# A transformer decoder layer on one core: q and k transposed without stacking, their rows spread by DMA inside SBUF

## What is computed

```python
x = x + attn(layernorm(x), Wqkv, Wo)          # rope on q and k, causal, 16 heads
x = x + xattn(layernorm(x), ctx, mask)        # softmax(x ctx^T / 16) ctx
x = x + ffn(layernorm(x), gate, w1, w2, w3, sw1, sw2, sw3)

q, k = rope(q), rope(k)                       # r0 = x0 cos - x1 sin, r1 = x0 sin + x1 cos
scores = where(causal, q k^T / sqrt(16), -inf)
out = softmax(scores) v
```

## Time and profile before

| | us |
|---|---|
| runs, median of 3 | 271.58 |
| runs, lowest to highest | 269.91 to 271.66 |
| profiled execution, span from first to last instruction | 271.7 |
| TensorE busy in it | 259.4 |
| ScalarE, VectorE, GpSimd busy | 174.8, 170.0, 122.4 |

### The profile page before, as it was taken

The page is one execution under the profiler, slowest core; times in us unless marked ns, Lnnn a source line. Parts: engine busy times, 40 slices in busy tenths (PEclk is TensorE's granted clock), DMA queues, the critical chain, the costliest instruction groups (busy, mean ns, idle before and its releaser), DMA issues.

```text
span 271.7 us, 4900 instructions
## 1 busy us (share of the span) xinstructions
PE 259.4 (95%) x1805; PEld 210.2 (77%) x1810; DVE 170.0 (63%) x361; ACT 174.8 (64%) x292; POOL 122.4 (45%) x133
## 2 busy tenths in 40 slices
PE   7888989999999999999989999999999999999994
PEld 2447756768877787868778888888989898888884
DVE  3675886867778666776852579638446634545453
ACT  7479379889967799888888855627565313222230
POOL 4447454988776918990954780334320000000000
PEclk9997999999999999999999999999999999999999
DMA  7891000000000000006609600000000079000002
GB/s 235 328 397 70 1 5 2 0 5 0 2 0 0 5 0 4 1 5 229 195 12 249 170 0 4 2 0 2 0 0 2 14 230 255 6 0 4 0 0 78
DMA packets 11879, 17.08 MB, mean 63 GB/s; under 512 B 1904, under 2 KB 8272, under 8 KB 11856
## 3 DMA queue, kind: packets, MB, share of 16 engines
q1 hardware_dynamic: 11856, 16.78, 19.6%
HBM read 15.63 MB, written 1.08 MB: 62 GB/s over the span
## 4 chain that ended last, share of the span: by engine, by line
PE 71%; POOL 8%; DMA 6%; DVE 6%; issue 4%; ACT 3%; SPq 2%; DVEq 0%; ACTq 0%
PE bank L789 26%; PE bank L898 13%; PE bank L802 11%; PE bank L951 4%; DMA res<-x 4%; POOL prob_lo L419 3%; DMA w_raw<-w 3%; PE bank L843 3%; PE bank L796 2%; PE bank L829 2%; PE bank L867 2%; PE bank L822 2%; PE bank L847 2%; POOL w_lo L426 1%; PE bank L824 1%
## 5 line engine op out<-in xcount | busy, mean ns | idle before, releaser
L419 POOL TENSOR_TENSOR prob_lo<-prob,prob_hi 128x1536 f16<-128x1536 f32 x16 | 49.9, 3120 | 14.9 <-ACT prob_hi L542 14.8
L789 PE MATMUL bank<-x_hi,w_hi 128*128 128x512 f32 x112 | 45.5, 406 | 0.0
L789 PE MATMUL bank<-x_hi,w_lo 128*128 128x512 f32 x112 | 44.2, 395 | 0.0
L789 PE MATMUL bank<-x_lo,w_hi 128*128 128x512 f32 x112 | 44.1, 393 | 0.0
L615 DVE TENSOR_REDUCE negm<-bank 128x2 f32<-128x512 f32 (+1 forms) x48 | 31.6, 685 | 8.6 <-PE bank L824 6.6
L771 DVE TENSOR_TENSOR h_lo<-h_c,h_hi 128x512 fp32r<-128x512 f32 x28 | 23.6, 845 | 21.0 <-ACT h_hi L581 20.8
L581 ACT CAST h_hi<-h_c 128x512 fp32r<-128x512 f32 x28 | 17.3, 617 | 24.6 <-DVE h_c L766 17.1
L757 DVE TENSOR_TENSOR h_c<-bank,h_s 128x512 f32<-128x512 f32 x28 | 19.3, 688 | 21.9 <-PE bank L789 18.3
L898 PE MATMUL bank<-w_hi,h_hi 128*128 128x256 f32 x112 | 32.9, 294 | 0.1
L575 ACT ACTIVATE h_s<-bank 128x512 f32<-128x512 f32 x28 | 16.7, 596 | 24.7 <-PE bank L789 24.7
L898 PE MATMUL bank<-w_hi,h_lo 128*128 128x256 f32 x112 | 31.6, 283 | 0.0
(11 more groups left out here) (128 smaller groups left out, 573.3 us busy)
## 6 DMA issues: line engine op xcount, KB each, us to landing
w_raw<-w SPq DMA_DIRECT2D x3, 1792.0 KB, 8.2
comb_b<-comb_dram SPq DMA_DIRECT2D x8, 256.0 KB, 4.9
res<-x SPq DMA_DIRECT2D x4, 256.0 KB, 7.0
ctxt_s<-ctx_t SPq DMA_DIRECT2D x4, 256.0 KB, 7.5
ctx_s<-ctx SPq DMA_DIRECT2D x4, 256.0 KB, 7.4
out<-res SPq DMA_DIRECT2D x8, 128.0 KB, 1.8
comb_b<-comb_dram SPq DMA_DIRECT2D x4, 224.0 KB, 4.8
wqkv_s<-wqkv SPq DMA_DIRECT2D x1, 768.0 KB, 4.8
```

The lines of the kernel that those rows point to most:

```text
L419: eng.tensor_tensor(prob_lo[:, b % 2], prob[:, b % 2], prob_hi[:, b % 2], ALU.subtract)\
L789: ins = pe.matmul(dst, a(k), c(k), start=(k == 0 and i == 0), stop=(k == kt - 1 and i == 2))
```

## The change

A tile's `rot` is transposed as it is: its 512 columns give four transposes instead of sixteen, into one PSUM bank (step `tr`, now one per tile). ScalarE casts that bank once to the high part `qk_hi`, VectorE subtracts once for the low part `qk_lo` (step `kt`). The steps `sh` are gone on both engines, and so is `stk`. To spread the rows into the stacked buffers, SP issues nine DMAs inside SBUF (step `sk`, function `shuffle`): six for q (16 partitions each) and three for k (32 each), six of the nine from the high part. `sk.0` and `sk.1` move a tile each of batch 0, `sk.2` to `sk.4` a whole batch each of batches 1 to 3. The maxima products of a batch now wait for all nine (`qk_in`), and w3's load for the last two moves. The columns of Wq and Wk are put in another order on the host so that a head's channels come out as `shuffle` needs them, and the rope products follow that order. A pair of heads takes 96 rows instead of 112. The row of ones in `k_t` is written once by a DMA. The diff, cut to its core; of the lists only SP's:

```diff
-SHIFT = SLOT + KROWS
+SHIFT = 2 * KROWS
+PIECES = ((0, 0), (1, 1), (2, 0)), ((0, 0), (1, 0), (2, 1))
+MOVES = 9
...
     "SP": """
-        ln1.0 mt.0 mt.1 mt.2 mt.3 mt.4 ct.0 mt.5 w3.0 ct.1 ro.0 ro.1 cb.0 ct.2 ct.3 y.0 cb.1 y.1
+        x.1 x.2 w1.0 w2.0 sk.0 sk.1 x.3 wo.0 cx.0 mt.0 cx.1 mt.1 sk.2 gt.0 mt.2 sk.3 ro.0 mt.3 sk.4 mt.4 ro.1 ct.0
+        w3.0 mt.5 ct.1 cb.0 ct.2 y.0 ct.3 cb.1 y.1
...
+            def shuffle(g):
+
+                b, tok = (0, slice(g * P, (g + 1) * P)) if g < NT else (g - 1, slice(0, S))
+                tile = g if g < NT else NT * b + 1
+                if g == 0:
+                    sp.wait_ge(s["zero_ok"], 2)
+                elif g == NT:
+                    sp.wait_ge(s["zero1_ok"], 2)
+                if b >= 2:
+                    sp.wait_ge(s["s_ps"], 3 * NG * (b - 1))
+                for low, src, ok in ((0, qk_hi, "hi_ok"), (1, qk_lo, "lo_ok")):
+                    sp.wait_ge(s[ok], tile + 1)
+                    for r in range(2):
+                        for a, piece in PIECES[0]:
+                            if piece == low:
+                                row = 2 * DH * a + DH * r
+                                sp.dma_start(q_t[row:row + DH, b % 2, :, r, tok].bitcast(F32),
+                                             src[P // 2 * r:P // 2 * (r + 1), b % 2, 0:2, tok].bitcast(F32))\
+                                    .then_inc(s[f"qk_in{g}"], 16)
+                    for a, piece in PIECES[1]:
+                        if piece == low:
+                            row = 2 * DH * a
+                            sp.dma_start(k_t[row:row + 2 * DH, b % 2, :, tok].bitcast(F32),
+                                         src[:, b % 2, 2:4, tok].bitcast(F32)).then_inc(s[f"qk_in{g}"], 16)
...
-                    sp.wait_ge(s["st_ps"], 4 * NT * B)
+                    sp.wait_ge(s["qk_in3"], 16 * MOVES)
+                    sp.wait_ge(s["qk_in4"], 16 * MOVES)
                     sp.dma_start(w3_raw[:], w3.rearrange("(f p) c -> p f c", p=P)).then_inc(s["w3_in"], 16)
...
+                    act.copy(qk_hi[:, n // NT % 2, :, n % NT * P:(n % NT + 1) * P],
+                             ps_st[n % 2][:].rearrange("p (g q) -> p g q", g=4)).then_inc(s["hi_ok"], 1)
...
+                    dve.wait_ge(s["hi_ok"], n + 1)
+                    dst = (slice(None), n // NT % 2, slice(None), slice(n % NT * P, (n % NT + 1) * P))
+                    dve.tensor_tensor(qk_lo[dst], ps_st[n % 2][:].rearrange("p (g q) -> p g q", g=4),
+                                      qk_hi[dst].bitcast(F32), ALU.subtract).then_inc(s["lo_ok"], 1)
...
-                    for j in range(4):
-                        h = 8 * c + 2 * j
-                        ins = pe.transpose(ps_st[c % 2][:, j * P:(j + 1) * P],
-                                           stk[:, n % 2, h:h + 2, :].bitcast(F32).rearrange("p h r -> p (h r)"), ident[:])
+                    for c in range(4):
+                        ins = pe.transpose(ps_st[n % 2][:, c * P:(c + 1) * P],
+                                           rot[:, n % 2, 2 * c:2 * c + 2].rearrange("p g a i -> p (g a i)"), ident[:])
...
                     if b == 0:
-                        pe.wait_ge(s["qt_ok"], 2)
-                        pe.wait_ge(s["kt_ok"], 2)
+                        pe.wait_ge(s["qk_in0"], 16 * MOVES)
...
                     elif b % FILLS == 0:
+                        pe.wait_ge(s[f"qk_in{b // FILLS + 1}"], 16 * MOVES)
+                        pe.wait_ge(s["lo_ok"], NT * (b // FILLS + 1))
```

More of the change, by code:

```diff
@@ L62 @@
+        ln3.3 w3.11 w3.12 w3.13
     """,
     "ACT": """
[L64 to L67, removed]
@@ new lines @@
+        m.15 s.8 s.9 m.16 m.17 pv.0 m.18 m.19 s.10 s.11 m.20 m.21 pv.1 m.22 m.23 mt.2 early.1 pv.2 tr.4 tr.5 s.12 pv.3
+        s.13 s.14 v.2 s.15 ot.0 s.16 s.17 wo.0 s.18 m.24 m.25 s.19 s.20 m.26 pv.4 m.27 m.28 t2.0 xt.3 m.29 xs.0 m.30
+        qk.6 pt.0 m.31 m.32 ro.0 s.21 m.33 s.22 s.23 pv.5 m.34 m.35 qk.7 mt.3 t3.0 tr.6 pv.6 late.1 lg.0 s.24 s.25
+        tr.7 pv.7 s.26 v.3 ct.0 s.27 ot.1 s.28 s.29 wo.1 s.30 pv.8 s.31 m.36 m.37 s.32 m.38 m.39 t2.1 m.40 m.41 xs.1
+        s.33 m.42 s.34 m.43 pt.1 pv.9 mt.4 ro.1 s.35 s.36 m.44 m.45 s.37 m.46 m.47 s.38 s.39 t3.1 s.40 pv.10 mt.5
@@ new lines @@
+        late.1 lg.1 s.41 up.0 s.42 pv.11 ct.1 s.43 up.1 ot.2 dn.0 wo.2 s.44 s.45 pv.12 up.2 pv.13 t2.2 s.46 s.47 xs.2
+        up.3 pt.2 dn.1 pv.14 ro.2 up.4 dn.2 up.5 t3.2 dn.3 up.6 lg.2 up.7 pv.15 dn.4 ct.2 up.8 ot.3 dn.5 wo.3 up.9
+        up.10 t2.3 dn.6 xs.3 dn.7 up.11 pt.3 dn.8 ro.3 dn.9 up.12 dn.10 dn.11 t3.3 up.13 up.14 up.15 lg.3 dn.12 dn.13
+        up.16 up.17 dn.14 ct.3 dn.15 up.18 up.19 dn.16 dn.17 up.20 dn.18 dn.19 up.21 up.22 up.23 dn.20 up.24 dn.21
+        dn.22 up.25 up.26 dn.23 up.27 dn.24 dn.25 dn.26 dn.27
@@ L315, in _ @@
                         .then_inc(s[f"shift_ok{b % 2}"], 16)
-                elif part == "ln1" and b == 0:
+                elif part == "x":
+                    load_x(b)
+                elif part == "sk":
+                    shuffle(b)
+                elif part == "w1":
+                    sp.dma_start(w1_raw[:], w1.rearrange("(k p) n -> p k n", p=P)).then_inc(s["w1_in"], 16)
+                elif part == "gt":
                     sp.dma_start(gate_raw[:], gate.rearrange("(k p) n -> p k n", p=P)).then_inc(s["gate_in"], 16)
                     sp.dma_start(mask_u8[:], mask[None, :, :].broadcast_to([P, B, S])).then_inc(s["mask_in"], 16)
-                    load_x(2)
+                elif part == "wo":
                     sp.dma_start(wo_s[:], wo.rearrange("(k p) n -> p k n", p=P)).then_inc(s["wo_in"], 16)
-                    load_x(3)
-                    load_ctx(0)
-                    load_ctx(1)
+                elif part == "cx":
+                    load_ctx(b)
+                elif part == "w2":
                     sp.dma_start(w2_raw[:], w2.rearrange("(k p) n -> p k n", p=P)).then_inc(s["w2_in"], 16)
@@ L462, in _ @@
             for i in range(2):
-                rows = slice(SLOT * i, SLOT * (i + 1))
-                act.copy(q_t[rows, 0, :, 1 - i, :], still[rows, None, 0:S].broadcast_to([SLOT, PAIRS, S]))\
+                act.copy(q_t[0:SHIFT, 0, :, i, :], still[0:SHIFT, None, 0:S].broadcast_to([SHIFT, PAIRS, S]))\
                     .then_inc(s["zero_ok"], 1)
@@ L1054 @@
     a = {k: np.asarray(v) for k, v in inputs.items()}
-    order = np.arange(C).reshape(H, DH // 2, 2).transpose(2, 0, 1).reshape(2, -1)
+    order = np.arange(C).reshape(4, 2, 2, DH // 2, 2).transpose(4, 1, 2, 3, 0).reshape(2, -1)
     columns = np.concatenate([order[0], C + order[0], order[1], C + order[1], 2 * C + np.arange(C)])
```

177 lines of the change are left out of this document (68 added, 109 removed).

## The result

| | us |
|---|---|
| changed kernel, median of 5 runs | 311.91 (310.31 to 314.02) |
| kernel before, same chip | 271.18 |
| ratio, 95% interval | 1.1525 (1.1486 to 1.1564) |
| profiled execution, span | 308.5 (before 271.7) |
| mean granted TensorE clock | 0.917 (before 0.994) |

Forecast were 263 us, a range of 255 to 279, and faster. It became 40.7 us slower.

What follows compares the result with a forecast made beforehand. No engine alone was taken to bound the attention stages; relieving four would shorten them. Batch 3's first maxima product at 99.0 us plus 163.5 us after it gave 262.5, said as 263, range 255 to 279.

Steps and rivals of the forecast that it cites:

- What goes: Work removed over the kernel: TensorE 10.6 us, ScalarE 23.7, VectorE 5.5, GpSimd 11.7; rope products and 96 rows cost nothing.
- D = 7.9 us: Time the DMA engines need for one batch's nine pieces, 1.57 MB at 199 GB/s: 7.9 us.
- The sign named for being wrong: The forecast counts as wrong if GB/s in the moves is near 100 or near 350.
- The upper bound of 11.8: A batch's pieces: six into 16 partitions at 100 GB/s, three into 32 at 199, together 11.8 us.
- The second rival: Batch moves: the rate halves again for 16 partitions, TensorE waits at every first maxima product, end 278 us; chance 0.32.
- Issue at 0.484 us: SP's queue: each small DMA takes 0.484 us to issue, 4.4 us a move, 22 us over five, costed at nothing.
- the moves would queue behind w2's load: At the start: w1 and w2 go ahead of the first move, 5.3 MB, so the half moves run from 18 us.
- ScalarE's evacuation did not wait long for w1: Tile 0 at the start: high parts at 15.1 us behind a w1 cast; a long wait would show the forecast wrong.
- Up to 1.7 us: In stalls of the slow-moves case: TensorE's clock falls to mostly the 1.2 GHz level, costing up to 1.7 us a stretch.
- From m.36 on 163.5 us: From batch 3's first maxima product to the end: 167.1 us before, less 0.6 and 3, so 163.5.
- the 3 us for the earlier w3: After batch 3's first maxima product: w3's load goes ahead of the last shift row, saving 3 us.
- The third rival: After batch 3's first maxima product: GpSimd's w_lo and prob_lo bind again, gains are lost, end 268 us; chance 0.12.

Runs made afterwards that it cites:

- h.15 moved: Changed kernel with rows at a step of 3, and GpSimd's last subtraction for the probabilities moved earlier in its list: 289.07 us, ratio 1.067 against the kernel before.

## Why the prediction was wrong

**What goes: right.** ScalarE 24.8 us less (23.7 forecast), GpSimd 13.0 (11.7), VectorE 3.7 (5.5; 7.0 with the collision gone). The rope products and the 96 rows cost nothing that shows. TensorE's 10.6 us are seen only roughly: at full clock, with products in all waits, it is busy 260.6 us against 259.4 before, of which products with zeros are 19.3 against 8.3, so some 10 less without them (an estimate, as they overlap others).

**D = 7.9 us for a batch's pieces: the step that failed.** It was taken from 199 GB/s in the earlier trace rows, a stretch of 0.70 us with pieces of 64 and 112 partitions under way, the DMA engines 0.83 busy. For pieces of 16 and 32 the measured rate is 117 to 125 GB/s, 13 us; m.12 stands 15.0 us behind the first issue, where 3.0 + 1.4 + 7.9 or less were summed, and TensorE waits 7.3, 6.9 and 7.1 us at m.12, m.24 and m.36. The sign named for being wrong, GB/s near 100, came. The upper bound of 11.8 was too low too, since 32 partitions were put at 199 GB/s and are no faster than 16. The second rival had the mechanism, at 0.32. With the rows spread the moves come to what had been forecast (10.1 us against 9.3), and that is worth 17.6 us.

**Issue at 0.484 us: too low.** The copies inside SBUF take 0.65 each by themselves and 0.69 in the kernel; with a quarter of the data a move still took 8.5 us to its use. At the start the issue is the bound: sk.1 is issued until 28.5, m.4 stands at 30.87 and not 26.7, and the DMA engines are only half busy there:

```profile
24.50:30.80 6.30, 3.05 (x20) 2.40 (x20) 3.21 (x6) 0.00 (x0) 1.27 (x1) 0.86 0.52 135
```

That the moves would queue behind w2's load was wrong: the first issue is at 16.0 and not 18, and w2 behind the moves gained nothing. ScalarE's evacuation did not wait long for w1, as forecast (qk_hi at 15.33, forecast 15.1).

**The clock: seen, but not summed.** "Up to 1.7 us" a stretch stood in the second rival alone, and the forecast's own waits of 2.4 us had no such price. Runs at full clock show 11.7 us where the waits were only 2.1 to 3.4 us long, and 10.6 for three of the long waits of the changed kernel. Slow moves were put at 278 for D = 11.8; at 4 us for each further us, D = 13 gives 283. Of the 29 us from there to 312, 16.5 are the collision and the clock: the narrow rows with h.15 moved and products in all waits take 295.4. Of the 12 left, 6.5 lie behind m.36 (170.0 us from m.36 at 124.70 to the end in that run, against 163.5) and the rest in the stretches ahead of it.

**From m.36 on 163.5 us: wrong.** 178.3 followed. With the collision and the low clock gone it is 167.9 from m.36's first maximum to the end, 166.1 before (from the profiled executions): the 3 us for the earlier w3 are not to be seen. The third rival looked to GpSimd's list too, but for waiting work; what cost time there was that GpSimd's subtraction kept VectorE out.

**Span and median.** The sum took the span of 271.7 for the median. In the run of the changed kernel a time is 1.8 us over its span (310.31 and 308.5), so the profiled execution of the kernel before was longer than its median. That is too little to explain the miss.

The sum by runs, all medians: 311.9 as changed; 17.6 less with the rows spread; 5.3 less with h.15 moved; 11.7 less at full clock; 277.4. What is left over the kernel before, 7.2 us on one chip, stays open. Moves that land 2 to 3 us late are the likely cause, but that is argued: more lead was tried only with fewer products or none, and not shown to take it off. Between the two profiles (spans 275.3 and 271.7), by VectorE's maxima, the stage that ends with m.12 is 3.4 us longer, batch 2's maxima 1.7 and what follows m.36 1.8, while the stages that end with m.24 and m.36 are 2.7 and 0.6 shorter.

## What to carry to other kernels

Before spreading rows by DMA inside SBUF, look at which partitions one transfer writes: where the order of the rows is free, put them at a step, not side by side. Price a wait of TensorE in front of dense products above its own length (in this kernel at about twice: 10.8 us of waits, 11.7 us of clock), and try products with zeros in it early. When a list is made anew, look for a GpSimd instruction beside a VectorE instruction with two SBUF operands: it shows as one instruction far over its median. It costs time only where somebody waits for it: 3.1 us here, next to nothing in the kernel before.

## What was not expected of the hardware

- 32 neighbouring partitions took 786 KB in 8.04 us, 16 in 8.77; 16 at a step of 8 in 5.69.
- Two queues writing to partitions far apart were no faster than one: 8.81 and 8.77 us.
- With the moves on another queue, the maxima's small DMAs took 4.6 and 4.9 us from issue to use, against 2.2 on the moves' own queue ahead of them.
- Issuing a copy inside SBUF took its queue 0.65 us in the copies alone and 0.69 in the kernel, one of the small loads of comb_b 0.48.
